# Two attention layers on one core: every part of P times V becomes the first item behind the scores of its step

## The reference

```
# layer 0
h = relu(layernorm(x))
q, k, v = heads(h @ Wq + bq), heads(h @ Wk + bk), heads(h @ Wv + bv)
scores = q k^T / sqrt(32) + beta * adj        # where adj > 0, else -9e15
x = x + softmax(scores) @ v
# layer 1
h = relu(layernorm(x))
q, k, v = heads(h @ Wq.T), heads(h @ Wk.T), heads(h @ Wv.T + bv)
scores = q k^T * 384**-0.5 + 2 * adj          # a row that is all zero counts as no row
x = x + (softmax(scores) @ v) @ Wo.T + bo
```

## Time and profile before

| what | value |
|---|---|
| median of three runs | 2030.54 us |
| profiled execution, its own time | 2028.77 us |
| its span | 2027.0 us |
| PE busy | 1903.3 us (94%) |
| PEld (weight loads) busy | 1227.1 us (61%) |
| DVE busy | 1835.6 us (91%) |
| ACT busy | 1669.7 us (82%) |
| POOL busy | 915.2 us (45%) |
| DMA, mean | 207 GB/s |
| mean granted TensorE clock | 0.989 |

### The profile page before, as it was taken

How to read it: one execution, slowest core, us unless ns; L and a number is a source line. 1 busy time by engine, 2 the same in 40 slices (tenths; PEclk the granted TensorE clock), 3 DMA queues, 4 the chain that set the end, 5 groups by cost and what they waited for, 6 DMA issues and landing times.

```text
span 2027.0 us, 49910 instructions
## 1 busy us (share of the span) xinstructions
PE 1903.3 (94%) x18288; PEld 1227.1 (61%) x18288; DVE 1835.6 (91%) x3992; ACT 1669.7 (82%) x4263; POOL 915.2 (45%) x1115
## 2 busy tenths in 40 slices
PE   5999999999999999997999999999999999999995
PEld 3565656666556566664666666666666666666663
DVE  5999999999999999997999999999999999999982
ACT  5998988999889889897888888888888878788771
POOL 6366654456565554561353334433344333443321
PEclk9999999999999999998999999999999999999997
DMA  3888889888888898889887788887887878877774
GB/s 131 199 212 217 223 213 244 212 221 214 218 219 224 226 236 221 220 211 222 205 224 195 187 221 207 204 202 188 221 208 201 200 190 218 213 200 199 176 195 134
DMA packets 105107, 419.07 MB, mean 207 GB/s; under 512 B 27216, under 2 KB 30800, under 8 KB 104864
## 3 DMA queue, kind: packets, MB, share of 16 engines
q1 hardware_dynamic: 77920, 307.60, 61.8%
q0 software_dynamic: 26944, 108.27, 19.0%
HBM read 88.61 MB, written 25.17 MB: 56 GB/s over the span
## 4 chain that ended last, share of the span: by engine, by line
PE 48%; DVE 21%; DMA 11%; ACT 11%; SPq 6%; issue 2%; POOL 1%; DVEq 0%; POOLq 0%
DVE s L337 11%; PE ring L246 11%; DMA pk<-pt 10%; PE sc L221 10%; PE out L300 9%; DVE pt L350 8%; PE ring L274 6%; SPq L182 6%; ACT s L459 5%; PE ring L253 4%; PE ring L235 4%; ACT xin L466 2%; PE ring L239 2%; ACT pl L483 1%; ACT wo L506 1%
## 5 line engine op out<-in xcount | busy, mean ns | idle before, releaser
L459 ACT ACTIVATE s<-s,nmax 128x512 f32<-128x512 f32 x1536 | 1094.9, 725 | 163.8 <-DVE nmax L337 163.7
L337 DVE CUSTOM_DVE_ANT_0 s<-sc,bias 128x512 f32<-128x512 f32 x1536 | 968.1, 686 | 74.5 <-PE sc L221 54.2
L350 DVE STREAM_TRANSPOSE pt<-s 128x2048 f32<-128x2048 f32 x288 | 663.7, 2305 | 0.5 <-issue 0.5
L221 PE MATMUL sc<-k,q 32*128 32x512 f32 x3072 | 439.7, 642 | 51.5 <-DVE nmax L337 38.9
L300 PE MATMUL out<-pk,v 128*32 128x192 f32 x6144 | 294.4, 333 | 36.8 <-DMA pk<-pt 36.8
L459 ACT ACTIVATION_READ_ACCUMULATOR s<-s,nmax 128x1 f32 x1536 | 310.7, 202 | 0.0
L300 PEld LDWEIGHTS out<-pk,v 128*32 128x32 f32 x6144 | 181.7, 111 | 175.9 <-issue 84.3
L253 PE MATMUL ring<-wv,hT 128*128 128x384 f32 x1152 | 237.6, 351 | 0.0
L246 PE MATMUL ring<-hT,wq 128*128 128x512 f32 x864 | 227.8, 408 | 1.5 <-DVE hT L365 1.5
L246 PE MATMUL ring<-hT,wk 128*128 128x512 f32 x864 | 228.0, 408 | 0.0
L221 PEld LDWEIGHTS sc<-k,q 32*128 32x128 f32 x3072 | 121.2, 183 | 164.9 <-DVE nmax L337 86.7
(11 more groups left out here) (85 smaller groups left out, 1971.7 us busy)
## 6 DMA issues: line engine op xcount, KB each, us to landing
pk<-pt SPq DMA_DIRECT2D x1536, 192.0 KB, 5.3
bias<-in_adj POOLq DMA_DIRECT2D x32, 1024.0 KB, 12.3
res<-in_x POOLq DMA_DIRECT2D x16, 768.0 KB, 15.0
x_between<-res POOLq DMA_DIRECT2D x16, 768.0 KB, 7.5
xin<-x_between POOLq DMA_DIRECT2D x16, 768.0 KB, 10.1
res<-x_between POOLq DMA_DIRECT2D x16, 768.0 KB, 10.5
out_x<-res POOLq DMA_DIRECT2D x16, 768.0 KB, 6.6
xin<-in_x POOLq DMA_DIRECT2D x15, 768.0 KB, 9.0
```

The source lines that it names most:

```text
L221: mm = nc.tensor.matmul(m.sc[:, j, :], m.q[rows, s % 2, P * t:P * (t + 1)], m.k[rows, s % 2, :], start=True, stop=True)
L337: nc.vector.tensor_tensor_reduce(out=m.s[:, t % 2, j, :], in0=m.sc[:, j, :], in1=m.bias[g % 2][:, t, :], scale=s_scale[layer], scalar=3.0e ...
L350: nc.vector.transpose(out=to, in_=m.s[:, t % 2].rearrange("p j (i a e) -> p (j i) a e", a=QUADS, e=HD)).then_inc(turned, 1)
L459: nc.scalar.activation(tile, tile, ACT.Exp, bias=m.nmax[s % 2][:, t, j:j + 1], scale=-1.0, accum_out=m.sums[s % 2][:, t, j:j + 1]).then_in ...
```

## The change

It changes the fractions of the `pv` places in both layers to .01, so that each part of P times V stands ahead of all other items of its step. No item changes its step.

```
--- before.py
+++ after.py
@@ -47,7 +47,7 @@
     "qk": (-2.90, -1.90, 1.10, 2.10, 4.27, 6.10),
     "v": (-3.50, -0.50, 0.50, 3.50),
     "tp": (3.31, 3.32, 3.33, 3.34, 7.31, 7.32, 7.33, 7.34, 11.31, 11.32, 11.33, 11.34),
-    "pv": (5.20, 6.20, 8.20, 9.20, 10.20, 12.20, 13.20, 14.20, 16.20),
+    "pv": (5.01, 6.01, 8.01, 9.01, 10.01, 12.01, 13.01, 14.01, 16.01),
     "post": (17.50, 17.60, 18.50, 20.60),
 }, {
     "hT": (-4.50, -4.40, -4.30),
@@ -56,7 +56,7 @@
     "sums": (0.40, 4.40, 9.40),
     "zero": (2.53, 6.40, 10.40),
     "tp": (3.31, 3.32, 3.33, 3.34, 7.31, 7.32, 7.33, 7.34, 11.31, 11.32, 11.33, 11.34),
-    "pv": (5.20, 6.70, 8.32, 9.20, 10.70, 12.32, 13.20, 14.70, 16.32),
+    "pv": (5.01, 6.01, 8.01, 9.01, 10.01, 12.01, 13.01, 14.01, 16.01),
     "spread": (7.30, 12.30, 16.61),
     "post": (17.50, 17.60, 18.50, 20.50),
 })
```

## The result

The changed kernel takes 2069.03 us, the median of four runs (2064.57 to 2075.44), against 2028.96 us before, there too the median of four (one more than the 2030.54 ahead of the prediction): the ratio is 1.0199, with a 95% interval of 1.0177 to 1.0222. It is slower by 40 us; 2076 us, 47 more, had been forecast. The profiled execution has a span of 2068.2 us, 41.2 more than before.

The account below looks back on a forecast made before the run. TensorE was taken to bind layer 1 (97% busy) and to be level with VectorE in layer 0. The profiled 2028.8 us plus 12 (layer 0) and 35 (layer 1) gave 2075.8, forecast as 2076, range 2050 to 2100.

Parts of the forecast that it names:

- The passed item: On TensorE, the item that P times V passes comes later by one part: 1.44 us (moved part) or about 1.0 (part 0).
- the place worked out as 1.24: Layer 0, steps 10 to 11: ScalarE's copy of k starts at 612.02 instead of 610.78, 1.24 us late.
- step 10: Layer 0, steps 10 to 11: late k copy delays exponentials, tp copies, fourth transposes and VectorE's scores; 0.95 us a graph.
- step 2: Steps 2 to 3, late k copy by the same path: 0.85 us in layer 0; 0.6 in layer 1 (steps 2 to 4).
- The fourth rival: Half price: ScalarE catches up before the tp copies, leaving only k's direct wait, 0.7 us in step 11; 2056 us, chance 0.13.
- Step 6: Layer 0, steps 6 to 7: ReLUs already hold back k's copy, so it comes only about 0.1 us late.
- Layer 1's post item: Layer 1, step 6: passed by P times V, it reaches VectorE 1.44 us late; less 0.8 slack, loss 0.65 us.
- The cover in layer 0: Step 4's 25.1 us of TensorE waits for moves of P absorb 22 of 28.5 us; later landings give back 5.
- The third rival: No cover: the moves land later by all that TensorE is later; 2096 us, chance 0.13.
- the first: Rival, transfers bind: part 1 comes before its half of the move lands, adding 42 us in layer 0; 2118 us, chance 0.08.
- The second rival: Headroom: TensorE's stalls are absorbed, as VectorE, 93 and 90% busy, is what counts; 2030 us, chance 0.05.
- The fifth rival: Faster: step 0's second half-move issued 0.6 us sooner in layer 1, layer 0's waits perhaps shrinking; 2014 us, chance 0.03.

Follow-up runs that it names:

- e2: Kernel before, with only part 0 first in steps 1 and 9, and layer 1's part 2 of step 0 ahead of the spread transposes: 2028.7 us, ratio 1.0022.
- e5: Changed kernel, with ScalarE's items of the step before one exponential later in the steps of tile 3: 2065.73 us, ratio 1.0183.
- e6: Changed kernel, with layer 1's part 1 of step 6 back behind k, zero and post item: 2053.91 us, ratio 1.013.
- e7: Kernel before, with layer 0's part 2 of the third chunk moved behind the q of its step: 2021.62 us, ratio 0.9961.
- e8: The whole change put on top of e7: 2081.01 us, ratio 1.0257.
- e11: e2 with the sums of layer 1's steps 0 and 9 right behind P times V again: 2032.7 us, ratio 1.0011.
- e4: Kernel before, with the change in layer 1 alone: 2065.3 us, ratio 1.0181.

## Why the prediction was right, step by step

**The rows read.** One comparison was wrong: the 34.1 us of layer 0 are VectorE's waits for scores, the 9.9 us of layer 1 TensorE's waits for VectorE, so they aren't the same row. VectorE's wait in layer 1 is 8.0 us and TensorE's in layer 0 20.6. Nothing in the sum hung on it.

**The passed item, and who reads it.** Right. ScalarE's waits for k are 36.9 and 57.1 us over the whole trace, 94 in all (70 to 110 said). They are 1.16 us at the place worked out as 1.24, and 1.54 in step 11 of layer 1, at 1566.44 us (1.44). q's delay costs nothing in layer 0 (e2). Nothing was gained by the earlier parts, as said: over the whole trace SyncE's queue waits for P times V 348.3 us instead of 574.9, but for VectorE's transposition of P 500.2 instead of 219.3. The earlier part only changes what the queue waits for.

**The end of a chunk: the sum right, its path half wrong.** 0.95 us was forecast for step 10 and 0.85 for step 2; VectorE's loss at the first is 0.85 in the graph shown, and TensorE's scores come 0.82 and 0.80 us later on average over the fourteen middle graphs. But the prediction called the direct wait of the scores for k's copy hidden, since VectorE needs those scores later, and laid the whole price on the late exponentials and the ring slot behind them. The rows after and e5 show the reverse: TensorE loses 0.78 us to the direct wait and the late transposes take 0.18 longer (2.18 us for 2.00), of which 0.06 reaches the scores behind the v item (619.88 - 615.02 = 4.86 us, and 616.80 - 612.00 = 4.80 before). "Hidden" was true of VectorE and false of TensorE: its next items start late as well, and the scores behind those are what VectorE waits for. The two paths run side by side and come out alike as both start from the same 1.2 us; that the forecast's path gave the right sum is in part luck. e5 takes most of the second path away and wins 0.17 us a chunk end. No run takes away the direct wait alone, so what the late exponentials would then cost isn't measured. The fourth rival had the direct wait (0.7 us), but counted too little beside it.

**Step 6.** Layer 0: 0.1 us was said, and the whole of what step 7 shows is under that. Layer 1's post item: 0.65 said, 0.64 measured (e6), with VectorE's 1.41 for 1.44.

**The cover in layer 0.** Right, and better than said. Of 25.1 us of waits 22 were to be covered and 5 given back by later landings; 19.8 went (25.1 - 5.3). TensorE comes to step 4 1.6 us later than before. Taking at most 1.6 us off each of the 14 waits of the trace before (0.55 to 3.48 us) gives 19.9 us, an estimate that leaves nothing for later landings; it agrees in the sum, not graph by graph. Gross, the chunk ends cost 0.85 + 0.8 + 0.1 us a graph, 26 us in 15 graphs; net of 19.8 that is 6. The forecast had 12. That it is a cover and not a low price is shown by step 4, which got 1.28 us shorter where all other steps together got 1.7 longer, and by e7 and e8: with most of the wait gone the same change costs 1.3 us a graph of layer 0 instead of 0.4. The third rival (no cover, 2096) is refuted in its mechanism, and so is the first: no wait for a first half appeared, as the six waits for `pk` that are left in layer 0 are all in step 4.

**Layer 1.** 2.2 us a graph was said, 2.24 measured. Errors cancel: steps 10 and 11 cost 0.88, not 0.95; step 2 costs 0.48, not 0.6 (from the scores of step 3 to those of step 5 it is 1515.90 to 1526.40 now and was 1492.79 to 1502.81), and the two places where the change of tiling mode was put at nothing cost 0.14 each, 0.28 a graph and some 4 us in all. That term had no price in the rows then; e11 shows one. The Trainium skill (TensorEngine Tiling (Array Packing), Key Properties) says that a change of the mode drains the engine. The rows agree with it in sign; what they show is 0.14 to 0.21 us a change. The second rival (headroom) is refuted for this kernel: with weight loads at 62% of layer 1 TensorE had no room for these waits, and layer 1 paid them in full (e4). The Trainium skill (Perfetto Trace Analysis, Identifying the Most-Contended Engine) has TensorE's headroom judged by its weight loads and not by matmul busy time. In layer 1 here that reading misleads, and the 97% of matmul busy time is the better sign. The fifth rival was to count only if the copies of k weren't late, and they were.

**The sum.** 12 + 35 were said; the layers alone give ratios of 1.0023 and 1.0181, 5 and 37 us. By the rows layer 0 cost 6 us, not 12. Five of these 6 are the later landings that didn't come; a gross cost and a cover each some 2 us smaller than said cancel. Layer 1 took 2 us more than said, and the last 2 us between the two layers' 42 and the whole change's 40 are within the intervals.

**The limits.** That ScalarE's order is what makes the copy of k late has been varied only by one exponential. A k projection issued a step earlier, with P times V first, wasn't tried. That the moves land no later when TensorE is later is inferred from the waits; the landings themselves weren't varied. e8 carries e7's own new wait for k's copy with it, so e7 and e8 aren't free of side effects.

## What to carry to other kernels

In a fixed queue the item that comes first is free only if the reader of the item it passes stands later in its own queue: look up that reader's place, and count each engine that starts late for it, not only the last one. A wait that exists pays for delays ahead of it; before such a change is called cheap, or the wait is removed, price both together. And where moving an item hides a wait, look at the next engine that reads what waited: e7 alone gave a third of what it gave once ScalarE's copy was moved too, and that second edit alone made the kernel slower.

## What the runs showed of the hardware

Two groups of matmuls of the same 128x32 tiling overlap by 0.19 us in the records, a full-array group and a 128x32 group by 0.08; with the 0.03 us by which the group's own row is longer this makes 0.14 us for each group that loses its like as a neighbour. Counted over whole steps with the same work and no waits, in layer 1's steps 0 and 9 of e2, the kernel before and e11, each change of tiling costs 0.14 to 0.21 us. The mean granted clock of the profiled runs was 0.986 to 0.992, and between 1500 and 1700 us, where the steady graphs of the kernels before and after were read, it was 1.00 in both, so those differences aren't the clock's.
